# Products of two neighbouring tokens shared through differences, in 64-column tiles, in the head of a one-core transformer block

## The chip, the core and the metric

One of the cores of a Trainium2 chip runs the kernel. The metric is the device time of one execution, in microseconds, from the runs' own clock; the trace adds, for one profiled execution, when each engine's instructions and each transfer ran.

## What is computed

The reference takes x (8 x 64 channels x 128 times x 64 variables), cuts the time axis into 16 overlapping patches of 16 steps at stride 8 (the last one repeats the edge value), applies a real FFT to each patch, and maps all frequencies and channels to 64 numbers per token with W:

```
patches = xp[:, :, idx, :]                     # 16 patches of 16, stride 8
xf = jnp.fft.rfft(patches, axis=-2, norm='ortho')
x_emb = jnp.concatenate([x_real, x_imag], axis=-1) @ W.T      # 8192 tokens x 64
h = _layernorm(h + _L0_attn_ref(h), axis=-1)   # attention over all 8192 tokens, one head of 64
h = _layernorm(h + _L0_ffn_ref(h, ...), axis=-1)    # 8 experts, two of them per token
```

FFT and W are linear, so the token embedding is one matrix per time step of a patch. The attention normalizes each token to length one (f) and needs softmax(f f^T) f over all 8192 tokens.

## The kernel before, in words

The program is written engine by engine with semaphores; nothing is scheduled by a tool, so the order in the code is the order on each engine. It has three parts: the head (x to tokens h, their norms and f), the score phase (512 tiles of scores), and the last part (experts and layer norms).

**Head.** VectorE first folds DFT and W into `weff`: for each of four taps s a matrix of 128 x 128 in f32. The 128 rows are 64 channels for the first and 64 for the second half of a stride of 8 time steps. Columns 0 to 63 are the weights that a block of 8 steps has as the first half of a patch, columns 64 to 127 those that it has as the second half of the patch before. TensorE multiplies x of one batch b (128 rows, 16 blocks m of 64 variables, per tap) with `weff` in `product(b, q, s)`: two halves q of 512 columns, four taps s, summed in PSUM, so 8 matmuls of 128x512 in f32 for each of 8 batches. `first_products` interleaves batches 0 and 1 with the arrival of the four taps, and fills waits with `kept_busy` matmuls on the identity. `products(b)` does b = 2 to 7. ScalarE copies the result into `prod` (L715). `tokens(i)` (L433) transposes it with the identity: token n is the upper half of block n plus the lower half of block n+1, so 16 transposes for 8 token columns, and VectorE's `tokens_out` (L929) sums pairs in PSUM into h. Block 16, the edge, is one matmul more (L442).

x comes in eight loads of 2 MB, each as two DMAs of 1 MB (rows 0 to 63 on SyncE's queue, 64 to 127 on ScalarE's), into a ring of three buffers; load b+3 waits until the products of b are done (`s_prod`). GpSimd loads the edge values `xedge` when x of batch 1 has landed.

For each group i of 8 token columns follow: squares on ScalarE (`h_squares`, L705), their sum and a maximum on VectorE (`norms`, L935, L936), the power -0.5 (L312) and f = h times it (L314) on GpSimd, the rounded f on ScalarE (`high_of_f`, L709), its rest on GpSimd (L316), a DMA transpose and two swaps on SyncE's queue (`transposed`, `swapped`) into `hilo` and `lohi`, which `scores` reads. VectorE also centres the bias b2 in the head and splits it into three parts (15 small operations, L912 to L924); `tokens` waits for `s_b2`, though only `down` in the last part uses the result.

**Score phase.** For each s of 512: `scores(s)` (12 matmuls on 64x64 tiles, L462), exp on ScalarE (L840), the low part of it on VectorE (`low_part`, L949), and the sums over values on TensorE (L479, L492). `tokens(6)` and `tokens(7)` are issued behind `scores(0)`. Small work is hung into single steps by tables (`LATE_HIGHS`, `LATE_NORMS`, `beside`).

**Last part.** The experts: `up` (L561), `expand`, `weigh` (L1090), `down` (L643, two matmuls of 128x64 weights on 512 columns of f32, which write the two halves of one PSUM bank).

## Time and profile before

| | |
|---|---|
| median of 3 runs | 877.54 us (876.84 to 877.97) |
| the profiled execution | 877.67 us, span 875.9 us |
| TensorE | 858.7 us busy, 98% of the span |
| VectorE | 764.8 us, 87% |
| ScalarE | 651.2 us, 74% |
| GpSimd | 167.8 us, 19% |
| granted TensorE clock | 0.997 of full speed |
| read from HBM | 18.21 MB |

The span runs from the first to the last instruction; 1.8 us of the profiled time lie around it. Busy shares are means over all stages, so a change in the head is judged from the head's own rows.

### The profile page before, as it was taken

To read this page: it belongs to the slowest core of one execution; us is meant where nothing else is said; L and a number is where in the kernel's file an instruction comes from. 1 tells how busy PE (TensorE), PEld (TensorE's weight loads), DVE (VectorE), ACT (ScalarE), POOL (GpSimd) and SP (SyncE) were. 2 spreads that over 40 slices of the span, in tenths; PEclk is the share of its full clock that TensorE was granted. 3 is DMA by queue.
4 is the path that set the end of the run, shared out by engine and by line. 5 is a ranking of instruction groups with operands and counts; after the bars stand their busy time and mean duration, and the time that the engine had idled before them with its cause. 6 is when DMAs were issued, how large, how long until landed. Compare 5 with 4: busy or idle time off the path is not lost.

```text
span 875.9 us, 30900 instructions
## 1 busy us (share of the span) xinstructions
PE 858.7 (98%) x13408; PEld 449.7 (51%) x13408; DVE 764.8 (87%) x915; ACT 651.2 (74%) x1271; POOL 167.8 (19%) x183
## 2 busy tenths in 40 slices
PE   7999999999999999999999999999999999999995
PEld 6444666765555555555555555555555555543331
DVE  5425999999899999999998999899889999989994
ACT  0125888788788878878887887787878778878873
POOL 0145330000120000000000000000000199958323
PEclk9999999999999999999999999999999999999998
DMA  9996320000000000000000000000000000000111
GB/s 285 231 288 118 48 62 3 3 3 3 2 3 2 2 3 2 3 3 2 3 2 3 2 2 3 2 3 2 3 2 2 4 2 2 3 1 1 33 29 37
DMA packets 31783, 26.48 MB, mean 30 GB/s; under 512 B 12576, under 2 KB 29472, under 8 KB 31648
## 3 DMA queue, kind: packets, MB, share of 16 engines
q1 hardware_dynamic: 22768, 15.38, 7.6%
q10 hardware_dynamic: 8752, 8.86, 3.7%
q8 instruction: 106, 1.74, 0.9%
q0 software_dynamic: 128, 0.26, 0.2%
q14 instruction: 29, 0.24, 0.1%
HBM read 18.21 MB, written 2.10 MB: 23 GB/s over the span
## 4 chain that ended last, share of the span: by engine, by line
PE 95%; DVE 2%; ACT 1%; issue 1%; DMA 0%; POOLq 0%; DVEq 0%; POOL 0%; ACTq 0%
PE ps L462 38%; PE ps L479 26%; PE ps L492 13%; PE ps L393 6%; PE ps L561 3%; PE ps L643 3%; PE ps L505 2%; PE ps L402 1%; DVE ring L1090 1%; PE ps L573 1%; DVE ring L949 1%; DMA f<-in_L_tok_W_dram 0%; ACT ring L806 0%; PE ps L433 0%; PE ps L386 0%
## 5 line engine op out<-in xcount | busy, mean ns | idle before, releaser
L949 DVE TENSOR_TENSOR ring<-ring 128x1024 f16<-128x1024 f32 x512 | 603.1, 1230 | 43.9 <-ACT ring L840 43.6
L840 ACT ACTIVATE ring<-ps 128x1024 f32<-128x1024 f32 x512 | 519.3, 1020 | 129.5 <-PE ps L462 129.3
L462 PE MATMUL ps<-big 64*64 64x512 f16 x6144 | 376.2, 376 | 0.9 <-ACT ring L840 0.9
L479 PE MATMUL ps<-ring,fs 64*64 64x512 bf16 x4096 | 275.7, 384 | 0.0
L462 PEld LDWEIGHTS ps<-big 64*64 64x64 f16 x6144 | 178.9, 106 | 156.2 <-ACT ring L840 3.8
L479 PEld LDWEIGHTS ps<-ring,fs 64*64 64x64 f16 x4096 | 120.8, 106 | 105.1
L492 PE MATMUL ps<-ring,fs 64*64 64x512 f16 x2048 | 154.7, 376 | 0.5 <-DVE ring L949 0.3
L840 ACT ACTIVATION_READ_ACCUMULATOR ring<-ps 128x1 f32 x512 | 101.3, 198 | 0.0
L339 POOL TENSOR_SCALAR stat<-stat 128x16 f32<-128x16 f32 (+2 forms) x4 | 2.9, 724 | 449.8 <-DVE stat L998 449.5
L492 PEld LDWEIGHTS ps<-ring,fs 64*64 64x64 f16 x2048 | 60.3, 107 | 51.8 <-issue 2.7
L393 PE MATMUL ps<-ring,weff 128*128 128x512 f32 x128 | 56.7, 596 | 0.1
L806 ACT ACTIVATE ring<-ps,b1s 128x512 f32<-128x512 f32 x64 | 40.4, 682 | 17.6 <-PE ps L561 17.4
L1090 DVE TENSOR_TENSOR ring<-ring,ps 128x512 f32<-128x512 f32 x64 | 40.9, 681 | 5.6 <-ACT ring L806 4.6
L393 PEld LDWEIGHTS ps<-ring,weff 128*128 128x128 f32 x128 | 23.7, 190 | 28.0 <-issue 27.5
L715 ACT ACTIVATE sums<-ps 128x1024 f32<-128x1024 f32 x8 | 8.2, 1024 | 39.7 <-PE ps L393 39.7
L561 PE MATMUL ps<-big,w1s 64*128 64x512 f32 x128 | 35.9, 637 | 0.4
L643 PE MATMUL ps<-ring,w2s 128*64 128x512 f32 x128 | 34.1, 611 | 0.9 <-DVE ring L1090 0.9
L929 DVE TENSOR_REDUCE h<-ps 128x512 f32<-128x1024 f32 x8 | 9.7, 1219 | 24.7 <-PE ps L433 24.7
L330 POOL TENSOR_TENSOR stat<-stat 128x16 f32<-128x16 f32 (+2 forms) x4 | 5.2, 1292 | 127.8 <-DVE stat L993 127.8
L316 POOL TENSOR_TENSOR fs<-f,fs 128x512 f16<-128x512 f32 x8 | 11.6, 1452 | 39.9 <-ACT fs L709 39.9
L505 PEld LDWEIGHTS ps<-cst,sums 128*128 128x128 f32 x128 | 15.5, 191 | 7.0 <-issue 6.9
L312 POOL TENSOR_TENSOR stat<-stat,cst 128x8 f32<-128x8 f32 x8 | 15.0, 1875 | 14.6 <-DVE stat L936 14.2
(144 smaller groups left out, 461.3 us busy)
## 6 DMA issues: line engine op xcount, KB each, us to landing
ring<-in_x_dram ACTq DMA_DIRECT2D x8, 1024.0 KB, 14.5
ring<-in_x_dram SPq DMA_DIRECT2D x8, 1024.0 KB, 13.6
big<-big SPq DMA_DIRECT2D x16, 128.0 KB, 2.4
out_dram<-h SPq DMA_DIRECT2D x14, 128.0 KB, 2.4
f<-in_L_tok_W_dram SPq DMA_DIRECT2D x1, 288.0 KB, 4.3
fs<-consts_dram ACTq DMA_DIRECT2D x1, 256.0 KB, 17.0
xedge<-in_x_dram POOLq DMA_DIRECT2D x2, 128.0 KB, 6.7
w1s<-in_L_ffn_w_dram SPq DMA_DIRECT2D x2, 128.0 KB, 9.3
```

The costliest lines, as they stand in the source:

```text
L312: gt(stat[:, INV_H, sl(i)], stat[:, LEAST, sl(i)], minus_half, ALU.pow).then_inc(s_rt, 1)
L393: return mm(bank(2 * (b % 2) + q).rearrange("p (m v) -> p m v", v=V), weff[:, s, :], xring[:, b % XR, 8 * q:8 * q + 8, s, :], start=(s == ...
L462: last = mm(bank(SLOT_BANK[slot_of(s)] + r)[m:m + 64, :], of_k[r][:, 128 * k + m:128 * k + m + 64], of_q[r][:, q0 + 512 * r:q0 + 512 * r + ...
L479: last = mm(bank(sums_bank(s // NT) + half)[m:m + 64, :], fs[64 * r:64 * r + 64, s % NT, m:m + 64], probs[64 * r:64 * r + 64, s % 8, :].bi ...
L492: last = mm(bank(sums_bank(s // NT) + half)[64 * e:64 * e + 64, :], fs[64 * r:64 * r + 64, s % NT, 0:64], probs_lo[64 * r:64 * r + 64, s % ...
L505: last = mm(part_bank(x, b)[:, (D + 1) * k:(D + 1) * (k + 1)], outT[:, 128 * t:128 * t + 128], centred_both, start=True, stop=True)
L561: last = mm(bank(r), w1s[rows, 128 * i:128 * i + 128], hT[rows, BLK * y:BLK * y + BLK], start=True, stop=True)
L643: last = mm(bank(4)[64 * n:64 * n + 64, :], w2s[:, i, :], hidc[:, (2 * u + n) % 4, :], start=False, stop=(i == NPAIR - 1), skip_group_chec ...
L806: a(hid[:, (2 * u + r) % 4, :], bank(r), ACT.Gelu, bias=b1s[:, u % 4:u % 4 + 1]).then_inc(s_gelu, 1)
L840: a(probs[:, s % 8, :], bank(SLOT_BANK[slot_of(s)], 2), ACT.Exp, accum_out=rowsum[:, s:s + 1]).then_inc(s_pr, 1)
L949: tt(probs_lo[:, s % 8, :], probs[:, s % 8, :], probs[:, s % 8, :].bitcast(BF16)[:, 1:2 * QC:2], ALU.subtract).then_inc(s_lo, 1)
L1090: tt(hidc[:, i, :], hid[:, i, :], bank(2 + r), ALU.mult).then_inc(s_hw, 1)
```

## The change

- Buffers: five for x instead of three. Slot 3 lies in the memory of f and fs, slot 4 in that of `big`, both needed later; batches 5, 6 and 7 reuse slots 0, 1, 2 behind the products of batches 0, 1, 2. Each slot has room for a 17th block, the edge, which ScalarE writes (`edge`). SyncE loads the experts' weights behind all transposes instead of ahead of them. `xedge` is loaded when x of batch 0 has landed.
- Products in tiles of 64 columns: `both_rows` (a tap in full) is four matmuls with 64 weight columns each. Upper PSUM rows get the even tokens, lower rows the odd ones, and both halves of a token are summed in PSUM.
- Sharing: with A and B the two weight halves, token 2j is A x[2j] + B x[2j+1] = A (x[2j] - x[2j+1]) + (A+B) x[2j+1], and token 2j+1 is B (x[2j+2] - x[2j+1]) + (A+B) x[2j+1]. The product with A+B (`wboth`) serves both. `shared_row` is two matmuls of 512 columns on the differences and two of 256 columns on the shared part. VectorE computes the differences, 1024 per partition and tap (`differences_of`). It is done for 22 of the 24 taps of batches 2 to 7; batches 0, 1 and tap 0 of batches 6, 7 go in full.
- `tokens` has 8 transposes for i = 0, 1 and 12 for the others; ScalarE copies out the shared part (`odd_out`), and VectorE copies (i < 2) or adds.
- Scaling: f for groups 0 to 3 is made by ScalarE in 8 operations (`f_of_h`), for 4 to 7 by GpSimd; the maximum goes from VectorE to GpSimd (`inverse_norm`).
- The b2 operations move from the head into steps t < 14 of q = 6 of the score phase (`b2_step`, one each).

Where nothing is shown, lines are left out.

```diff
...
-LATE_HIGHS = {12: 5, 22: 6, 30: 7}
+LATE_HIGHS = {5: 4, 13: 5, 25: 6, 34: 7}
...
+XR = 5
+XLEN = (NM + 1) * HALF * V
+X_SLOT = (0, 1, 2, 3, 4, 0, 1, 2)
+X_TURN = (1, 1, 1, 1, 1, 2, 2, 2)
+X_BEHIND = {5: 1, 6: 2, 7: 3}
+SHARED_TAPS = [(), ()] + 4 * [(0, 1, 2, 3)] + 2 * [(1, 2, 3)]
+SHARED = [(b, s) for b in range(B) for s in SHARED_TAPS[b]]
...
+            even = x_at(b)[:, 0:NM:2, s, :]
+            return bass.AP(even.tensor, even.offset, (even.ap[0], even.ap[1], even.ap[1][:1] + (2,), even.ap[2]))
+
+        def differences(s):
+            piece = (h[:, NT - 2 * G:NT, :].rearrange("p j o -> p (j o)"), sums[:, NTOK - 2048:NTOK - 1024], sums[:, NTOK - 1024:NTOK],
+                     big[:, NTOK - 1024:NTOK])[s]
+            return piece.rearrange("p (j e v) -> p j e v", j=NM // 2, e=2)
...
             for b in range(B):
-                if b >= XR:
-                    sp.wait_ge(s_prod, b - XR + 1)
...
+                if X_SLOT[b] == 3:
+                    sp.wait_ge(s_wfold, 1)
+                if b in X_BEHIND:
+                    sp.wait_ge(s_prod, X_BEHIND[b])
+                sp.dma_start(x_at(b)[0:64, 0:NM].rearrange("p m s v -> p m (s v)"),
+                             x_h[b, 0]).then_inc(s_xb[X_SLOT[b]], 16)
+            sp.wait_ge(s_prod, X_SLOT.index(4) + 1)
+            for i in range(NG):
+                transposed(i)
+            swapped(NG - 1)
...
-            pool.wait_ge(s_xb[1], 16)
-            pool.wait_ge(s_xc[1], 16)
+            pool.wait_ge(s_xb[0], 16)
+            pool.wait_ge(s_xc[0], 16)
...
+            def inverse_norm(i):
+                pool.wait_ge(s_ss, i + 1)
+                pool_ts(stat[:, LEAST, sl(i)], stat[:, SUM_HH, sl(i)], 1e-24, None, ALU.max).then_inc(s_least, 1)
+                pool.wait_ge(s_least, i + 1)
+                gt(stat[:, INV_H, sl(i)], stat[:, LEAST, sl(i)], minus_half, ALU.pow).then_inc(s_rt, 1)
+
+            inverse_norm(0)
             for i in range(NG):
-                pool.wait_ge(s_ss, i + 1)
-                gt(stat[:, INV_H, sl(i)], stat[:, LEAST, sl(i)], minus_half, ALU.pow).then_inc(s_rt, 1)
-                pool.wait_ge(s_rt, i + 1)
-                gt(f[:, sl(i), :], h[:, sl(i), :], wide(stat[:, INV_H, sl(i)]), ALU.mult).then_inc(s_f, 1)
+                if i + 1 < NG:
+                    inverse_norm(i + 1)
+                if i + 1 >= NG // 2 and i + 1 < NG:
+                    pool.wait_ge(s_rt, i + 2)
+                    gt(f[:, sl(i + 1), :], h[:, sl(i + 1), :], wide(stat[:, INV_H, sl(i + 1)]), ALU.mult).then_inc(s_f, 1)
                 pool.wait_ge(s_fhi, i + 1)
                 gt(fs[:, sl(i), D:2 * D], f[:, sl(i), :], fs[:, sl(i), 0:D], ALU.subtract).then_inc(s_fs, 1)
...
-            def product(b, q, s):
-                return mm(bank(2 * (b % 2) + q).rearrange("p (m v) -> p m v", v=V), weff[:, s, :],
-                          xring[:, b % XR, 8 * q:8 * q + 8, s, :], start=(s == 0), stop=(s == HALF - 1))
+            def u_bank(b):
+                return bank(2 * (b % 2))
+
+            def both_rows(b, s):
+
+                x_b, out_b = x_at(b), u_bank(b)
+                first, second = weff[:, s, 0:D], weff[:, s, D:2 * D]
+                reach = NM // 2 if b >= 2 else NM // 2 - 1
+                mm(out_b[0:64, :], first, x_b[:, 0:NM:2, s, :], start=(s == 0), stop=False, skip_group_check=True)
+                mm(out_b[64:128, :], first, x_b[:, 1:NM:2, s, :], start=(s == 0), stop=False, skip_group_check=True)
+                mm(out_b[0:64, :], second, x_b[:, 1:NM:2, s, :], start=False, stop=(s == HALF - 1), skip_group_check=True)
+                return mm(out_b[64:128, 0:V * reach], second, x_b[:, 2:1 + 2 * reach:2, s, :], start=False,
+                          stop=(s == HALF - 1), skip_group_check=True)
+
+            def shared_row(b, s):
+
+                pe.wait_ge(s_diff, SHARED.index((b, s)) + 1)
+                x_b, out_b, d = x_at(b), u_bank(b), differences(s)
+                first_one = s == SHARED_TAPS[b][0]
+                for e in range(2):
+                    last = mm(out_b[64 * e:64 * e + 64, :], weff[:, s, D * e:D * e + D], d[:, :, e, :],
+                              start=(s == 0), stop=(s == HALF - 1), skip_group_check=True)
+                last.then_inc(s_taken, 1)
+                for e in range(2):
+                    last = mm(bank(2 * (b % 2) + 1)[64 * e:64 * e + 64, 0:256], wboth[:, s, :], x_b[:, 1 + 2 * e:NM:4, s, :],
+                              start=first_one, stop=(s == HALF - 1), skip_group_check=True)
+                return last
...
-                    for q in range(2):
-                        last = product(b, q, s)
+                    both_rows(b, s)
                     if s == HALF - 1:
-                        last.then_inc(s_prod, 1)
+                        if b == 0:
+                            pe.wait_ge(s_xe, 32)
+                            pe.wait_ge(s_wpad, 1)
+                        mm(u_bank(b)[64:128, V * (NM // 2 - 1):V * NM // 2], wpad[:, :], xedge[:, b, :], start=False, stop=True,
+                           skip_group_check=True).then_inc(s_prod, 1)
...
-                for q in range(2):
-                    for s in range(HALF):
-                        last = product(b, q, s)
+                if b == 2:
+                    pe.wait_ge(s_wboth, 1)
+                for s in range(HALF):
+                    last = shared_row(b, s) if s in SHARED_TAPS[b] else both_rows(b, s)
                 last.then_inc(s_prod, 1)
...
-                pe.wait_ge(s_padev, 1)
-                pe.wait_ge(s_b2, 1)
+                if i == 1:
+                    pe.wait_ge(s_b2o, 1)
...
+                if bp >= 1:
+                    for k in range(n0 // 4, n0 // 4 + 2):
+                        for r in range(2):
...
-            pe.wait_ge(s_xe, 32)
-            pe.wait_ge(s_wpad, 1)
...
             def load(b):
...
+            for b in range(3):
                 load(b)
...
+            load(3)
+            load(4)
...
+            def edge(b):
+                a(x_at(b)[:, NM, :, :], xedge[:, b, :].unsqueeze(1).to_broadcast([128, HALF, V]), ACT.Copy).then_inc(s_edge, 1)
...
+            def odd_out(i):
...
+                of_rows = bank(4 + i % 2 * 2, 2).rearrange("p (r k o) -> p r k o", r=2, o=D)[:, :, 4:6, :]
+                a(odd_part[i % 2].rearrange("p (k r) o -> p r k o", r=2), of_rows, ACT.Copy).then_inc(s_odd, 1)
...
+            def f_of_h(i):
...
+                for j in range(G * i, G * i + G):
+                    last = a(f[:, j, :], h[:, j, :], ACT.Copy, scale=stat[:, INV_H, j:j + 1])
+                last.then_inc(s_f, 1)
...
+            act.wait_ge(s_xe, 32)
+            for b in range(2, B - 1):
+                edge(b)
             for b in range(B):
                 act.wait_ge(s_prod, b + 1)
-                if b + XR < B:
-                    load(b + XR)
-                a(prod[:, b // 2, 0:NM, b % 2, :], bank(2 * (b % 2), 2).rearrange("p (m v) -> p m v", v=V),
+                for later in X_BEHIND:
+                    if X_BEHIND[later] == b + 1:
+                        load(later)
+                used = 12 if b >= 2 else 8
+                a(prod[:, b // 2, 0:used, b % 2, :], bank(2 * (b % 2), 2)[:, 0:V * used].rearrange("p (k v) -> p k v", v=V),
                   ACT.Copy).then_inc(s_prodev, 1)
                 if b == 1:
-                    act.wait_ge(s_pad, 1)
-                    a(prod[:, :, NM, :, :], bank(7).rearrange("p (b c v) -> p b c v", c=2, v=V),
-                      ACT.Copy).then_inc(s_padev, 1)
-                if b >= 2 and b % 2 == 0:
+                    act.wait_ge(s_b2c, 1)
+                    a(b2f[:, 0, :], b2_rows, ACT.Copy).then_inc(s_b2o, 1)
+                if b == 2:
+                    edge(7)
+                    h_squares(0)
+                    h_squares(1)
+                if b in (4, 6):
+                    odd_out(b - 2)
+                    odd_out(b - 1)
+                if 3 <= b <= 6:
+                    f_of_h(b - 3)
+                    high_of_f(b - 3)
+                if b in (4, 6):
                     h_squares(b - 2)
-                    if b >= 3:
-                        high_of_f(b - 3)
...
+                if s == 1:
+                    odd_out(NG - 2)
+                    odd_out(NG - 1)
...
+            red(wpad[:, :], weff[:, :, D:2 * D].rearrange("p s k -> p k s"), AX.X, ALU.add).then_inc(s_wpad, 1)
+            tt(wboth[:, :, :], weff[:, :, 0:D], weff[:, :, D:2 * D], ALU.add).then_inc(s_wboth, 1)
...
+            def differences_of(b, s):
+
+                if s == SHARED_TAPS[b][0]:
+                    dve.wait_ge(s_xb[X_SLOT[b]], 16 * X_TURN[b])
+                    dve.wait_ge(s_xc[X_SLOT[b]], 16 * X_TURN[b])
+                    dve.wait_ge(s_edge, b - 1)
+                if (b - 1, s) in SHARED:
+                    dve.wait_ge(s_taken, SHARED.index((b - 1, s)) + 1)
+                odd = x_at(b)[:, 1:NM:2, s, :].unsqueeze(2).to_broadcast([128, NM // 2, 2, V])
+                tt(differences(s), x_around(b, s), odd, ALU.subtract).then_inc(s_diff, 1)
...
-                red(h[:, 8 * i:8 * i + 8, :], bank(4 + i % 2 * 2, 2).rearrange("p (s n o) -> p n o s", s=2, o=D),
-                    AX.X, ALU.add).then_inc(s_h, 1)
+                own = bank(4 + i % 2 * 2, 2).rearrange("p (r j o) -> p j r o", r=2, o=D)[:, 0:4]
+                to = h[:, 8 * i:8 * i + 8, :].rearrange("p (j r) o -> p j r o", r=2)
+                if i < 2:
+                    cp(to, own).then_inc(s_h, 1)
+                else:
+                    dve.wait_ge(s_odd, i - 1)
+                    tt(to, own, odd_part[i % 2].unsqueeze(2).to_broadcast([128, 4, 2, D]), ALU.add).then_inc(s_h, 1)
...
-                then(red(stat[:, SUM_HH, sl], squares[:, i % 2], AX.X, ALU.add))
-                ts(stat[:, LEAST, sl], stat[:, SUM_HH, sl], 1e-24, None, ALU.max).then_inc(s_ss, 1)
...
+                red(stat[:, SUM_HH, sl], squares[:, i % 2], AX.X, ALU.add).then_inc(s_ss, 1)
+
+            for s in range(HALF):
+                differences_of(2, s)
+            for b in (3, 5, 7):
+                taps = SHARED_TAPS[b]
+                for s in taps[:-2]:
+                    differences_of(b, s)
+                tokens_out(b - 3)
+                differences_of(b, taps[-2])
                 tokens_out(b - 2)
-                norms(b - 2)
+                differences_of(b, taps[-1])
+                norms(b - 3)
+                if b < B - 1:
+                    taps = SHARED_TAPS[b + 1]
+                    differences_of(b + 1, taps[0])
+                    norms(b - 2)
+                    for s in taps[1:]:
+                        differences_of(b + 1, s)
+            norms(B - 3)
...
-                if q == NG // 2 + 1 and t == 18:
+                if q == NG // 2 + 1 and t == 14:
                     w2_centred()
+                if q == NG // 2 + 2 and t < 14:
+                    b2_step(t)
```

TensorE's stream from batch 2 on, before: (weff is the weights, ring holds x, x2 and xc2 are the two halves of the load).

```order
L393 MATMUL ps<-ring,weff 128x512 [waits s_prodev,s_xc2,s_x2]
L393 MATMUL ps<-ring,weff 128x512 x7
L433 MATMUL ps<-cst,sums 128x64 [waits s_b2,s_padev,s_prodev]
L433 MATMUL ps<-cst,sums 128x64 x15
```

The same place now; h, sums and big hold the differences of taps 0, 1 to 2 and 3:

```order
L449 MATMUL ps<-h,weff 64x512 [waits s_prodev,s_wboth,s_edge,s_diff,s_xc2,s_x2]
L449 MATMUL ps<-h,weff 64x512
L453 MATMUL ps<-ring,wboth 64x256 x2
L449 MATMUL ps<-sums,weff 64x512 [waits s_diff]
L449 MATMUL ps<-sums,weff 64x512
L453 MATMUL ps<-ring,wboth 64x256 x2
```

Each tap is two products of 512 and two of 256 columns, 64 weight columns wide, and waits for its difference.

VectorE from batch 3 on, now. Before, only L929, L935 and L936 stood here, group by group:

```order
L1023 TENSOR_TENSOR h<-both_f 128x1024 [waits s_edge,s_taken,s_xc3,s_x3]
L1023 TENSOR_TENSOR sums<-both_f 128x1024 [waits s_taken]
L1030 COPY h<-ps 128x512 [waits s_tr]
L1023 TENSOR_TENSOR sums<-both_f 128x1024 [waits s_taken]
L1030 COPY h<-ps 128x512 [waits s_tr]
L1023 TENSOR_TENSOR big<-both_f 128x1024 [waits s_taken]
L1038 TENSOR_REDUCE stat<-squares 128x8 [waits s_sqf]
L1023 TENSOR_TENSOR h<-big 128x1024 [waits s_edge,s_taken,s_xc4,s_x4]
L1038 TENSOR_REDUCE stat<-squares 128x8 [waits s_sqf]
```

The tokens' copies and the sums of squares stand between the differences, and each waits for TensorE or ScalarE.

ScalarE's start, now; before, the two loads into `both_f` and `big` were not there, and its loads of batches 3 and 4 came behind the first products:

```order
L762 DMA ring<-in_x_dram 64x16x256 x3
L767 DMA both_f<-consts_dram 128x512
L768 DMA cst<-consts_dram 128x134
L762 DMA both_f<-in_x_dram 64x16x256
L762 DMA big<-in_x_dram 64x16x256
L772 ACT_TABLE_LOAD
L772 ACTIVATE rsmall<-cst 128x1 [waits s_cst]
L775 ACTIVATE ring<-rtmp 128x256 [waits s_xe]
```

The edges (L775) stand behind the issue of both loads.

## Rows read from the trace of the kernel before

**Rows 1.** The page: busy times, and the chain that ended last by engine.

```profile
PE 858.7 (98%) x13408; PEld 449.7 (51%) x13408; DVE 764.8 (87%) x915; ACT 651.2 (74%) x1271; POOL 167.8 (19%) x183
PE 95%; DVE 2%; ACT 1%; issue 1%; DMA 0%; POOLq 0%; DVEq 0%; POOL 0%; ACTq 0%
```

**Rows 2.** Chain of work in the head and behind it: start, us, what.

```profile
31.14 0.86 PE ps L442 x2
...
32.36 7.06 PE ps L393 x16
...
40.66 14.20 PE ps L393 x32
54.86 1.15 PE ps L433 x32
...
71.07 7.08 PE ps L393 x16
78.15 0.02 issue
78.17 1.03 ACT sums L715
...
80.00 2.36 DVE h L929 x2
```

**Rows 3.** Chain in the last part: L643, two f32 matmuls of 64 columns.

```profile
792.25 0.86 PE ps L643 x4
...
795.13 1.01 PE ps L643 x4
```

**Rows 4.** Stretches: us, then busy PE, PEld, DVE, ACT, POOL; clock, DMA share, GB/s.

```profile
16.00:22.00 6.00, 6.00 (x31) 3.85 (x30) 5.74 (x12) 0.61 (x2) 0.40 (x1) 1.00 1.10 348
26.00:31.00 5.00, 5.00 (x13) 2.13 (x13) 0.00 (x0) 0.93 (x1) 0.61 (x1) 1.00 0.26 40
31.00:68.00 37.00, 36.90 (x145) 16.91 (x144) 12.86 (x27) 9.77 (x14) 13.54 (x11) 1.00 1.11 290
603.00:641.00 38.00, 38.00 (x700) 19.68 (x696) 34.84 (x31) 30.85 (x59) 0.00 (x0) 1.00 0.01 2
641.00:690.00 49.00, 49.00 (x876) 25.81 (x872) 43.40 (x43) 38.59 (x77) 0.00 (x0) 1.00 0.01 3
```

**Rows 5.** VectorE: L949 by duration (ns, min/median/max), and one after another in time.

```profile
L949 DVE TENSOR_TENSOR ring<-ring x512: 1162/1221/2184, 82.3 to 772.7; 128x1024 f16<-128x1024 f32 x171
...
91.07 5.76 DVE L949 TENSOR_TENSOR ring<-ring 128x1024 f16<-128x1024 f32 x5
```

**Rows 6.** Groups of the whole span and of 14.9 to 78 us: busy, mean ns, idle before.

```profile
L1090 DVE TENSOR_TENSOR ring<-ring,ps 128x512 f32<-128x512 f32 x64 | 40.9, 681 | 5.6 <-ACT ring L806 4.6
...
L935 DVE TENSOR_REDUCE stat<-squares 128x8 f32<-128x512 f32 x6 | 4.1, 686 | 4.2 <-ACT squares L705 4.2
L715 ACT ACTIVATE sums<-ps 128x1024 f32<-128x1024 f32 x7 | 7.2, 1024 | 37.6 <-PE ps L393 37.6
```

**Rows 7.** GpSimd and VectorE beside each other, in time: start, us.

```profile
58.03 1.15 POOL L316 TENSOR_TENSOR fs<-f,fs 128x512 f16<-128x512 f32 x1 [4.12 <-ACT fs L709]
58.18 1.02 DVE L936 TENSOR_SCALAR stat<-stat 128x8 f32<-128x8 f32 x1
...
59.29 1.63 POOL L312 TENSOR_TENSOR stat<-stat,cst 128x8 f32<-128x8 f32 x1
...
108.62 2.14 POOL L316 TENSOR_TENSOR fs<-f,fs 128x512 f16<-128x512 f32 x1 [6.44 <-ACT fs L709]
...
109.66 2.18 DVE L949 TENSOR_TENSOR ring<-ring 128x1024 f16<-128x1024 f32 x1
```

**Rows 8.** ScalarE, in time: a load's issue, four scalings, a copy.

```profile
2.52 5.66 ACTq L691 DMA_DIRECT2D ring<-in_x_dram  x1
8.22 5.90 ACTq L696 DMA_DIRECT2D fs<-consts_dram  x1
...
790.40 1.05 ACT L762 ACTIVATE f<-f,stat 128x64 f32<-128x64 f32 x4
```

More of the change, by code:

```diff
@@ L170, in tower, with x_at, x_around @@
         b1s = sb("b1s", [128, NPAIR], F32)
+        def x_at(b):
+            if X_SLOT[b] < 3:
+                slot = ring[:, X_SLOT[b] * XLEN:(X_SLOT[b] + 1) * XLEN]
+            else:
+                slot = (both_f if X_SLOT[b] == 3 else big)[:, 0:XLEN]
+            return slot.rearrange("p (m s v) -> p m s v", m=NM + 1, s=HALF)
+        def x_around(b, s):
+            even = x_at(b)[:, 0:NM:2, s, :]
[4 more added lines that the diff above has]
+            return piece.rearrange("p (j e v) -> p j e v", j=NM // 2, e=2)
         hT = big[:, 0:NTOK // 2]
@@ L270, in _ @@
                     sp.dma_start(b1s[rows], b1[half:E:2].rearrange("i k -> k i")).then_inc(s_w1r, 16)
-            for i in range(NG):
-                transposed(i)
-            swapped(NG - 1)
             for w, (g, p0, p1) in enumerate(PIECES):
@@ L690, in load @@
             def load(b):
-                act.dma_start(xring[64:128, b % XR, :, :, :].rearrange("p m s v -> p m (s v)"),
-                              x_h[b, 1]).then_inc(s_xc[b % XR], 16)
-            for b in range(XR):
+                act.dma_start(x_at(b)[64:128, 0:NM].rearrange("p m s v -> p m (s v)"),
+                              x_h[b, 1]).then_inc(s_xc[X_SLOT[b]], 16)
+            for b in range(3):
                 load(b)
@@ L1013, in w2_centred, with b2_step @@
                 tt(w2s[:, :, :], w2s[:, :, :], wide(rsmall[:, 6, 0:NPAIR], NPAIR), ALU.add).then_inc(s_w2c, 1)
+            def b2_step(k):
+                if k == 0:
+                    dve.wait_ge(s_b2o, 1)
+                    dve.wait_ge(s_self, 32)
+                    then(red(rsmall[:, 5, 0:1], b2f[:, 0, :], AX.X, ALU.add))
+                if k == 1:
+                    then(ts(rsmall[:, 6, 0:1], rsmall[:, 5, 0:1], -1.0 / D, None, ALU.mult))
+                if k == 2:
+                    then(ts(b2f[:, 0, :], b2f[:, 0, :], rsmall[:, 6, 0:1], None, ALU.add))
+                if k in (3, 5, 7):
+                    then(cp(b2p[:, k // 2 - 1, :], b2f[:, k // 2 - 1, :]))
+                if k in (4, 6):
+                    then(tt(b2f[:, k // 2 - 1, :], b2f[:, k // 2 - 2, :], b2p[:, k // 2 - 2, :], ALU.subtract))
+                n = (k - 8) // 3
+                at = PARTS * n
+                if k in (8, 11):
+                    then(ts(b2f[:, 3, :], b2p[:, 0, :], part_mask[:, at:at + 1], None, ALU.mult))
+                if k in (9, 12):
+                    then(stt(b2f[:, 3, :], b2p[:, 1, :], part_mask[:, at + 1:at + 2], b2f[:, 3, :], ALU.mult, ALU.add))
+                if k in (10, 13):
+                    then(stt(b2s[:, n, :], b2p[:, 2, :], part_mask[:, at + 2:at + 3], b2f[:, 3, :], ALU.mult, ALU.add))
+                if k == 13:
+                    nc.vector.engine_nop().then_inc(s_b2, 1)
             def final_variance(w):
```

80 lines of the change are left out of this document (35 added, 45 removed).

## The prediction

> **What bounds the kernel now.** The page comes first: TensorE is busy for 98% of the span and makes 95% of the chain that ended last [rows 1]. So whatever shortens TensorE's stream shortens the kernel, unless something else becomes late. The change touches the head, and there the chain is read piece by piece [rows 2]. Each batch's products take 7.06 to 7.08 us (16 records; an f32 matmul of 512 columns is two), two batches take 14.20, a pair of token groups takes 1.15 for 32 transposes, and the first scores come at 78.15. These pieces follow each other without a gap, so before 78.15 no load and no other engine is waited for from batch 2 on. Third, the stretches [rows 4] tell what will be waited for next: from 16 to 22 us the DMA engines are full at 348 GB/s, from 26 to 31 nearly idle (share 0.26, because three buffers are full), from 31 to 68 full again at 290 GB/s. The loads end only some 10 us ahead of the head. I take 0.2% (1.75 us) as what a measurement can tell from no change.
>
> **TensorE's stream.** A full tap of a batch is four records of 7.06/16 = 0.441 us, 1.77 us. In 64 columns a tap in full is as many streamed columns on half the array, twice: the same 1.77 if two tiles run side by side. A shared tap has 512 and 256 columns instead of twice 512, so 0.75 of it, 1.32. 22 taps x 0.44 = **9.7 us** less. That tiles of 64 columns in f32 run side by side is seen in `down`: two such matmuls of 512 columns take 0.86 to 1.01 us [rows 3], not the 1.77 that they would take in turn. The bounds come from the same two rows. At 0.86 a full tap costs 1.72 and nothing changes for the worse. At 1.01 a full tap costs 2.02 (10 of them, +2.5) and a shared one 1.52 (22, -5.5), and only 3.0 are left. I take 0.88, the price of one full-width matmul, since 1.01 belongs to a group whose neighbours use other tile shapes, and here 16 to 32 records of one shape stand in a row.
>
> Transposes: 96 in the head become 64 (16, 24, 24), at 1.15/32 = 0.036 us each, -1.15. The edge matmul's 0.86 [rows 2] becomes two of 64 columns, at the price of a few transposes, -0.7. Sum -11.5: TensorE alone would be through at **66.6** instead of 78.15.
>
> **What TensorE now waits for.** VectorE makes 22 differences of 1024 f32 elements. The nearest row is L949, two inputs of 1024: 1.22 us as median, and (5.76 - 1.22)/4 = 1.14 from start to start when they follow each other [rows 5]. That is 25.1 us. Between them stand six `tokens_out` of 512 from PSUM (0.64 to 0.68 as L1090) and four sums of squares (0.69 as L935) [rows 6], 6.7 us. They start when x of batch 2 is there, about 26.5, and the last product follows by 1.3: 26.5 + 25.1 + 6.7 + 1.3 = 59.6. So VectorE has 7 us of room in sum, though in places little: over a pair of batches it needs 8 x 1.14 + 2.7 = 11.8 us and TensorE 8 x 1.32 + 0.86 = 11.4. Its lead is the four differences of batch 2, made while TensorE does batches 0 and 1.
>
> GpSimd takes some of this room. Beside VectorE's L936 its subtraction L316 held VectorE until its own end (58.18 + 1.02 = 59.20, against 58.03 + 1.15), and an L949 took 2.18 instead of 1.22 beside another L316 [rows 7]. Three subtractions fall into the new stretch: 3 x 0.96 = 2.9 us, and VectorE would be through at 62.5, still ahead.
>
> Loads: five are left behind batch 2, 10.5 MB, and 0.26 MB of edge values. At the 290 GB/s of the stretch 31 to 68 they take 37 us, at the 348 of the stretch 16 to 22, where only x was under way, 31 [rows 4]. They now follow on the third load at 26 instead of 31, so the last x lands at 57 to 63; the weights' many small pieces are out of the way, and I take 62.5. From then TensorE needs one full and three shared taps, 5.7, and VectorE, which must make three differences with two `tokens_out` between and be 1.3 ahead of the end, 3.4 + 1.35 + 1.3 = 6.1. The head ends at **68.6**: 9.5 us earlier, of which TensorE would have given 11.5. The missing 2 us are a wait for x of batch 7.
>
> **Behind the head.** On the chain stand ScalarE's copy (1.03) and VectorE's two reductions, 2.36 [rows 2]. The copy has 12 of 16 blocks (-0.2), the transposes are 24 of 32 (-0.3), and the reductions become two additions of 0.65 (-1.1). They wait for ScalarE's first exp and `odd_out`, which come about 1.2 later than the transposes. Net -0.4.
>
> **Costed at nothing.** ScalarE's new work (per group 8 scalings, 1.05/4 = 0.26 each or 2.1 us [rows 8], five edges ahead of batch 2, the odd parts) lies in the 37.6 us that it waits for products [rows 6]. If that cover were gone, the copies of products would be late and each would cost its own length. The transposes on SyncE's queue go ahead of the weights, whose first reader is far behind; hilo and lohi of group 0 are ready about 62 to 64, and `scores(0)` needs them at 68. For later groups the score phase gives 10 us per group. The 15 b2 operations, 3.3 us, leave a place where VectorE idled; in q = 6 they meet 38.0 - 34.84 = 3.2 us of idle time in the first 38 us, and 5.6 in the next 49 [rows 4], with eight buffers of scores between. Bounds 0 and 3.3; taken as 0.
>
> **Sum.** -9.5 - 0.4 = -9.9. The profiled execution becomes 877.67 - 9.9 = 867.8; it lies 0.13 above the median of 877.54, so on the median 867.6. I say **867.7**.
>
> **Rivals.**
> - *Late supply* (0.17): x of batch 7 lands later than 63, or ScalarE is held up. For it: a load's issue held ScalarE for 5.66 and then 5.90 us [rows 8], since its queue was full, and two more loads are now issued ahead of the edges and of the first copy of products. If the second is taken only after 31, differences of batch 2 begin 5 us late and VectorE's 59.6 + 2.9 become 67.5, with local waits on top. Against it: the third load was taken at 8.18, and the queues drain 2 MB in 7 us. It gives a head end of 70.5 to 73: 870 to 872.
> - *Tile overhead* (0.06): each pair costs 1.01. 3.0 instead of 9.7, so 874. The Trainium skill's page TensorEngine Tiling (section "Tiling Modes") says that changing the tiling mode drains the engine. Here shapes change only around `kept_busy` and `tokens`, where they changed before too, and the group of [rows 3] stands amid such changes.
> - *GpSimd's lock for every operation* (0.05): the powers too (L312, 1.63 [rows 7]) hold VectorE for their whole length, four in the head, +6.5 on 62.5 = 69, and with local waits 71: 870. Against it: over 512 executions, many of them beside GpSimd, L949's median stays at 1.22 [rows 5]. The Trainium skill's page SBUF — State Buffer (section "SBUF: two separate sides") says that a VectorE operation with two SBUF inputs and a GpSimd operation lock each other out for the whole instruction. The trace agrees for GpSimd's operations on 512 elements (2.18 beside 1.22) and shows no such length beside the small ones.
> - *VectorE becomes the bound, slower* (0.05): a difference reads three strided patterns in f32 and writes f32, where L949 writes f16. VectorE's chain ends at 26.5 + 22 d + 8.0 + 2.9 = 37.4 + 22 d. It decides from d = 1.33 against 66.6 and loses everything from d = 37.4 to 78.5, **d = 1.87**. At the 2.18 of L949's slowest [rows 5] the head ends at 85.4, 6.9 late: 884. Against it: L949, L935 and L1090 all take about one element per ns, whatever their patterns and types.
> - *The sharing does not come into effect* (0.02): products wait on loads throughout, as x arrives at one batch per 7 us, about what TensorE needs now. Then only the 5 us of idle DMA at 26 to 31 come back: -5, 872.5. That is inside the range too.
>
> **How the numbers follow.** The forecast (865.4 to 869.5) has 0.65: from its bounds, TensorE never waiting (-11.9, so 865.6) and x at 63.5. The supply, lock and full-bandwidth rivals reach to 872.5 and hold 0.24. Left outside are part of the tile overhead and the slow VectorE, 0.11, and what none of them names. The range is 865.4 to 872.8. Faster by over 0.2%: 0.93; within: 0.02; slower: 0.05.
>
> **What would show it.** On TensorE's chain, batches 2 to 5 take 5.3 us each with 2 x 2 records of 512 and 2 x 2 of 256 columns per tap, 6 and 7 take 5.7, and about 2 us of wait in front of batch 7 are ended by a load. The first scores start near 68.6. Differences last 1.2 us, some 2.1 beside GpSimd. The DMA share stays near 1.1 from 8 to 62. The step on loads is wrong if TensorE waits for differences instead; the step on tiles, if a pair of 512-column matmuls takes over 0.95; the whole, if the first scores move by much more than the end of the kernel does.

## The result, and the profile after

The changed kernel takes **872.35 us** (median of 5 runs, 870.29 to 873.77), the kernel before 877.63 (876.84 to 877.97, 5 runs beside them). The ratio is 0.9942, interval 0.9931 to 0.9954: 5.1 us faster. The forecast was 867.7 in a range of 865.4 to 872.8. The sign and the range held, the range by 0.45 us at its upper end, but about half of the expected gain is missing.

The page of the profiled execution (872.53 us, span 870.7), to be held against [rows 1]:

```profile
PE 850.0 (98%) x13498; PEld 438.8 (50%) x13498; DVE 782.9 (90%) x929; ACT 660.2 (76%) x1315; POOL 183.3 (21%) x187
PE 93%; DVE 2%; ACT 2%; issue 2%; DMA 0%; POOLq 0%; DVEq 0%; ACTq 0%; POOL 0%
```

TensorE's share of the chain fell from 95% to 93%, and "issue" rose from 1% to 2%: there are now waits on the chain. The chain in the head shows one of 5.18 us (start, us, what), where [rows 2] had none:

```profile
32.09 1.01 PE ps L449 x4
33.09 0.43 PE ps L453 x4
33.53 0.86 PE ps L449 x4
...
37.63 0.60 ACT sums L810
38.23 0.12 ACTq L762
38.34 5.18 issue
43.52 0.81 ACT sums L810
...
44.53 0.63 ACT squares L781
...
45.79 1.21 DVE h L1023
```

A shared tap is L449 (512 columns, four records, 0.86 or 1.01) and L453 (256 columns, 0.43), 1.29 in all; 1.32 was forecast. The timeline of TensorE gives the starts of the batches and the idle time in front of an instruction, in brackets:

```profile
32.02 1.08 PE L449 MATMUL ps<-h,weff 128*64 128x512 f32 x4
...
38.28 0.71 PE L500 MATMUL ps<-cst,sums 64*128 64x64 f32 x16 [0.88 <-ACT sums L810]
38.92 1.08 PE L449 MATMUL ps<-h,weff 128*64 128x512 f32 x4
...
47.15 1.08 PE L449 MATMUL ps<-h,weff 128*64 128x512 f32 x4 [2.85 <-DVE h L1023]
48.03 0.65 PE L453 MATMUL ps<-big,wboth 128*64 128x256 f32 x4
48.79 1.98 PE L449 MATMUL ps<-sums,weff 128*64 128x512 f32 x4
...
51.40 1.29 PE L449 MATMUL ps<-sums,weff 128*64 128x512 f32 x4
...
52.95 1.02 PE L449 MATMUL ps<-big,weff 128*64 128x512 f32 x4
...
54.34 0.46 PE L500 MATMUL ps<-cst,sums 64*128 64x64 f32 x8
...
55.23 1.08 PE L449 MATMUL ps<-h,weff 128*64 128x512 f32 x4
...
67.17 0.64 PE L437 MATMUL ps<-ring,weff 128*64 128x512 f32 x1
...
73.34 0.84 PE L532 MATMUL ps<-big 64*64 64x512 f16 x12
```

The first scores (L532) stand at 73.34. In the same view of the kernel before they stand at 78.06, so the head is 4.7 us shorter, and the profiled execution is 5.1 us shorter. What TensorE lost against a stream of 1.29 us per shared tap without gaps: 0.88 ahead of the transposes; 2.85 ahead of batch 4; 2.03 in batch 4, which ran from 47.15 to 54.34, 7.19 instead of 4 x 1.29 = 5.16; 0.21 in batch 5; 0.54 in batch 7 (67.17 to 73.34, 6.17 instead of 1.76 + 3 x 1.29 = 5.63). Sum 6.5, and 73.3 - 6.5 = 66.8.

Who was late is seen in ScalarE's timeline:

```profile
30.08 0.57 ACTq L762 DMA_DIRECT2D ring<-in_x_dram  x1
30.69 0.60 ACT L810 ACTIVATE sums<-ps 128x512 f32<-128x512 f32 x1 [4.09 <-PE ps L475]
31.80 5.79 ACTq L762 DMA_DIRECT2D ring<-in_x_dram  x1
37.63 0.60 ACT L810 ACTIVATE sums<-ps 128x512 f32<-128x512 f32 x1 [6.34 <-PE ps L453]
37.68 5.79 ACTq L762 DMA_DIRECT2D ring<-in_x_dram  x1
...
43.52 0.81 ACT L810 ACTIVATE sums<-ps 128x768 f32<-128x768 f32 x1 [5.18 <-issue]
```

VectorE, in the same view:

```profile
45.19 0.69 DVE L1038 TENSOR_REDUCE stat<-squares 128x8 f32<-128x512 f32 x1 [2.85 <-ACT squares L781]
45.79 1.21 DVE L1023 TENSOR_TENSOR h<-big 128x1024 f32<-128x1024 f32 x1
...
47.52 2.35 DVE L1023 TENSOR_TENSOR sums<-big 128x1024 f32<-128x1024 f32 x2
```

ScalarE issues its half of load 6 (rows 64 to 127) ahead of the copy of batch 1, and that of load 7 ahead of the copy of batch 2. Each issue holds it for 5.79 us, where that of load 5 takes 0.57. So the copy of batch 1 starts at 37.63 instead of at about 31.8, and the copy of batch 2 at 43.52. ScalarE's squares come behind that copy, VectorE's sum of squares (L1038) waits for them, and behind it in VectorE's order stands the difference of batch 4, tap 0, for which TensorE waits. The bracket at 37.63 names L453, a product of batch 2; the copy needs the products of batch 1, which were through before 32.02, when batch 2 began. So it was the issue that held it.

The stretches (columns as in [rows 4]):

```profile
31.00:40.00 9.00, 8.12 (x61) 3.70 (x59) 6.60 (x7) 1.00 (x3) 0.00 (x0) 1.00 1.09 346
...
47.15:48.00 0.85, 0.85 (x4) 0.37 (x6) 0.85 (x2) 0.00 (x0) 0.81 (x1) 1.00 1.10 349
48.00:50.00 2.00, 1.90 (x10) 0.71 (x8) 2.00 (x3) 1.10 (x5) 1.96 (x2) 0.63 1.09 348
50.00:52.00 2.00, 2.00 (x8) 0.71 (x6) 2.00 (x2) 1.54 (x5) 1.95 (x1) 0.52 1.09 345
52.00:60.00 8.00, 8.00 (x68) 3.64 (x66) 5.63 (x8) 4.92 (x14) 2.41 (x3) 1.00 1.09 251
60.00:68.00 8.00, 8.00 (x66) 3.60 (x64) 5.34 (x6) 4.88 (x14) 7.83 (x6) 1.00 0.10 24
601.00:640.00 39.00, 39.00 (x704) 20.43 (x700) 37.95 (x43) 30.89 (x60) 0.00 (x0) 1.00 0.01 3
```

Behind the wait of 2.85 us TensorE's granted clock is 0.63 and then 0.52, so near 1.2 instead of 2.4 GHz for a while. That is 1.6 of the 2.03 us of batch 4: the taps that start at 48.79 and 51.40 take 2.61 and 1.55 instead of 1.29. The first tap of batch 4 ran before, at a clock of 1.00 (47.15 to 48.00); it takes 1.64 to the start of the next, since that next one waits for the second difference, which VectorE makes from 47.52 to about 48.7. Loads run at 345 to 348 GB/s and are through by 60. In q = 6 (601 to 640) VectorE is busy for 37.95 of 39 us and TensorE for all of it.

### The profile page after: what moved, and what is told of

It reads as the page before. It is cut to its first block, busy times and chain, and to the rows that moved or that the text cites. A ratio compares the mean times of both kernels' runs of the same rounds, so it can differ in the third digit from the quotient of the medians.

```text
span 870.7 us, 31169 instructions
## 1 busy us (share of the span) xinstructions
PE 850.0 (98%) x13498; PEld 438.8 (50%) x13498; DVE 782.9 (90%) x929; ACT 660.2 (76%) x1315; POOL 183.3 (21%) x187
## 3 DMA queue, kind: packets, MB, share of 16 engines
q8 instruction: 107, 1.75, 0.8%
## 4 chain that ended last, share of the span: by engine, by line
PE 93%; DVE 2%; ACT 2%; issue 2%; DMA 0%; POOLq 0%; DVEq 0%; ACTq 0%; POOL 0%
PE ps L532 38%; PE ps L549 26%; PE ps L562 13%; PE ps L631 3%; PE ps L714 3%; PE ps L575 2%; PE ps L449 2%; PE ps L463 1%; ACT ring L943 1%; PE ps L453 1%; PE ps L437 1%; DVE ring L1232 1%; PE ps L643 1%; PE ps L439 1%; ACT ring L906 0%
## 5 line engine op out<-in xcount | busy, mean ns | idle before, releaser
L532 PE MATMUL ps<-big 64*64 64x512 f16 x6144 | 376.3, 376 | 1.3 <-ACT ring L943 0.9
L549 PE MATMUL ps<-ring,both_f 64*64 64x512 bf16 x4096 | 275.3, 384 | 0.0
L532 PEld LDWEIGHTS ps<-big 64*64 64x64 f16 x6144 | 176.1, 106 | 159.5 <-ACT ring L943 5.5
L549 PEld LDWEIGHTS ps<-ring,both_f 64*64 64x64 f16 x4096 | 119.1, 106 | 106.8
L562 PE MATMUL ps<-ring,both_f 64*64 64x512 f16 x2048 | 154.3, 376 | 0.1
L562 PEld LDWEIGHTS ps<-ring,both_f 64*64 64x64 f16 x2048 | 59.7, 107 | 51.9 <-issue 1.9
L810 ACT ACTIVATE sums<-ps 128x768 f32<-128x768 f32 (+1 forms) x8 | 6.1, 756 | 22.6 <-PE ps L453 13.3
L341 POOL TENSOR_SCALAR stat<-stat 128x8 f32<-128x8 f32 x8 | 12.1, 1518 | 34.1 <-DVE stat L1038 34.1
L575 PE MATMUL ps<-cst,sums 128*128 128x65 f32 x128 | 17.7, 281 | 0.0
L862 ACT ACTIVATE both_f<-both_f,stat 128x64 f32<-128x64 f32 x64 | 17.3, 341 | 0.0
L353 POOL TENSOR_TENSOR both_f<-both_f 128x512 f16<-128x512 f32 x8 | 15.9, 1987 | 4.5 <-ACT both_f L799 4.5
```

Of the source, the lines that this page charges most:

```text
L532: last = mm(bank(SLOT_BANK[slot_of(s)] + r)[m:m + 64, :], of_k[r][:, 128 * k + m:128 * k + m + 64], of_q[r][:, q0 + 512 * r:q0 + 512 * r + ...
L549: last = mm(bank(sums_bank(s // NT) + half)[m:m + 64, :], fs[64 * r:64 * r + 64, s % NT, m:m + 64], probs[64 * r:64 * r + 64, s % 8, :].bi ...
L562: last = mm(bank(sums_bank(s // NT) + half)[64 * e:64 * e + 64, :], fs[64 * r:64 * r + 64, s % NT, 0:64], probs_lo[64 * r:64 * r + 64, s % ...
L575: last = mm(part_bank(x, b)[:, (D + 1) * k:(D + 1) * (k + 1)], outT[:, 128 * t:128 * t + 128], centred_both, start=True, stop=True)
L862: last = a(f[:, j, :], f[:, j, :], ACT.Copy, scale=stat[:, OF_S, j:j + 1])
```

## The experiments

My theory after this reading was that the held issues and the clock behind the wait cost the missing 4.7 us (872.35 - 867.7), and that the sharing itself works as reckoned. Rivals: the gain comes from the earlier loads alone; the loads are the bound; VectorE and GpSimd hold each other.

**The issues taken from ScalarE** (e1_loads_on_sp; base: the change)

```diff
                 sp.dma_start(x_at(b)[0:64, ...], x_h[b, 0]).then_inc(s_xb[X_SLOT[b]], 16)
+                if b in X_BEHIND:
+                    sp.dma_start(x_at(b)[64:128, ...], x_h[b, 1]).then_inc(s_xc[X_SLOT[b]], 16)
...
-                for later in X_BEHIND:
-                    if X_BEHIND[later] == b + 1:
-                        load(later)
```

> The changed kernel with both halves of the loads of batches 5, 6 and 7 issued on SyncE's queue; ScalarE issues none of them. Theory (A): the changed kernel loses its missing gain because the issue of the loads of batches 6 and 7 holds ScalarE for 5.79 us each (31.80 and 37.68), so the copies of batches 1 and 2 and the squares of group 0 come late, TensorE idles 0.9 and 2.85 us and then runs at half clock from 48 to 52. Then the first scores come at 67 to 69 instead of 73.3 and the time is 866 to 868.5. Rival (B): VectorE's chain with its local waits is the bound anyway; the first scores stay after 72 and the time at 871 or more. Rival (C): one queue for both halves carries less than two; x of batch 6 or 7 becomes late and TensorE waits for a load, 869 to 872.

Measured: 880.99 us (878.99 to 881.85), ratio 1.0041 (1.0028 to 1.0053). The copy of batch 2 came in time, at 36.54. But the loads became slow (stretch 44 to 48, and the clock behind TensorE's waits from 52 on):

```profile
44.00:48.00 4.00, 3.11 (x18) 1.34 (x20) 4.00 (x5) 2.65 (x9) 2.65 (x3) 1.00 1.13 197
...
52.00:60.00 8.00, 5.32 (x18) 2.35 (x20) 6.42 (x7) 3.68 (x11) 0.17 (x1) 0.60 1.14 195
```

The DMA engines are as full as before (share 1.13) and move 197 GB/s instead of 347. Holding ScalarE is cured, and a worse wait, for x, takes its place; the first scores come at 81.07. That is the mechanism of rival C at a higher price than it named. So this run does not decide on the theory. Whether one queue or one half of the rows at a time is slow is taken up in the last experiment.

**TensorE kept busy ahead of batch 4** (e2_busy_wait; base: the change)

```diff
                 loaded(b)
+                if b == 4:
+                    for i in range(24):
+                        mm(bank(7)[:, 256:384], ident, ident, start=True, stop=True)
```

> The changed kernel with 24 matmuls of the identity (128x128) in front of the products of batch 4, so that TensorE works through its wait for the first difference. If the granted clock of 0.63 and 0.52 between 48 and 52 us comes from the idle 2.85 us before it, it stays at 1.00 there, batch 4 takes about 1.8 us less and the time is 870 to 871.5 with less spread between runs. If the drop has another cause, it stays and the time is 872 to 873.5 (the 24 matmuls fill only idle time).

Measured: 872.98 us (872.38 to 873.43), ratio 0.9951 (0.9938 to 0.9963), the same as the change. TensorE's timeline:

```profile
44.02 5.62 PE L484 MATMUL ps<-cst 128*128 128x128 f32 x48
49.58 1.08 PE L449 MATMUL ps<-h,weff 128*64 128x512 f32 x4
...
54.89 0.46 PE L503 MATMUL ps<-cst,sums 64*128 64x64 f32 x8
```

The clock stays at 1.00 in every stretch from 26 to 76, and batch 4 takes 54.89 - 49.58 = 5.31 us instead of 7.19. So the drop of the clock came from the wait. Of the 1.88 us, 0.30 are not the clock's: the filler also gave VectorE time, and the second difference is ready. The filler is 2.4 us too long (batch 4 begins at 49.58 instead of 47.15), which eats the gain; the time alone lies where the rival had it, and the trace is what decides.

**Loads 3 to 7 held back as with three buffers** (e3_three_at_once; base: the change)

```diff
-X_BEHIND = {5: 1, 6: 2, 7: 3}
+X_BEHIND = {3: 1, 4: 2, 5: 3, 6: 4, 7: 5}
...
-            load(3)
-            load(4)
```

> The changed kernel with loads 3 to 7 held back as three buffers would hold them (3 behind the products of batch 0, 4 behind batch 1 and so on), the same slots. It tells what the early loads are worth. Theory: no issue of a load holds ScalarE, but the DMA engines idle from 26 to 31 and every x comes 5 us later or waits for products; TensorE waits for loads, the first scores come at 72 to 76, time 871 to 875. Rival: if early loads bring nothing and the hold is all, the first scores come at 68 to 70 and the time is 867 to 869.

Measured: 877.11 us (876.56 to 879.54), ratio 1.0007 (0.9997 to 1.0016).

```profile
26.00:31.00 5.00, 5.00 (x30) 3.09 (x26) 1.97 (x2) 0.60 (x1) 0.61 (x1) 1.00 0.14 25
...
40.00:44.00 4.00, 0.79 (x2) 0.33 (x4) 2.16 (x2) 0.00 (x0) 0.00 (x0) 0.50 1.10 348
```

The DMA engines idle from 26 to 31 (25 GB/s), x of batch 3 is there at 41.8, TensorE waits 5.55 us, and the clock falls to 0.50 behind it. The first scores stand at 77.31. From load 3 on every issue on ScalarE takes 0.56 or 0.57 us, yet nothing is gained: all of the change together is worth nothing while x comes as late as before. What sharing alone is worth under these loads was not run.

**The loads on SyncE, without sharing** (e4_not_shared; base: the first experiment)

```diff
-SHARED_TAPS = [(), ()] + 4 * [(0, 1, 2, 3)] + 2 * [(1, 2, 3)]
+SHARED_TAPS = 8 * [()]
```

and the differences, the shared columns of the copy, their transposes and `odd_out` dropped.

> The kernel of the first run of this call without sharing: all 24 taps of batches 2 to 7 in full, four matmuls of 64 columns, no differences on VectorE, no shared part. It tells what sharing is worth. Theory: TensorE's stream grows by 22 x 0.44 = 9.7 us and nothing else is waited for, so the first scores come at 75 to 77.5 and the time is 875 to 877. Rival: if the loads bound the head instead, it grows by less than 5 us over the first run.

Measured: 879.54 us (877.81 to 880.5), ratio 1.0026 (1.0017 to 1.0035), 1.5 us less than with sharing, at intervals that overlap. The first scores come at 79.27, where the first experiment had them at 81.07; the 9.7 us more that the theory expected did not come. TensorE waits for loads ahead of batches 6 and 7 here too, since it has the slow loads of the first experiment. It says only that while TensorE waits for such loads the sharing gains nothing.

**The same issues, later in ScalarE's order** (e6_late_issue; base: the change)

```diff
                 act.wait_ge(s_prod, b + 1)
-                for later in X_BEHIND:
-                    if X_BEHIND[later] == b + 1:
-                        load(later)
+                if b == 0:
+                    load(5)
...
                   ACT.Copy).then_inc(s_prodev, 1)
+                if b == 2:
+                    load(6)
+                if b == 3:
+                    load(7)
```

> The changed kernel with ScalarE's half of load 6 issued behind the copy of batch 2 and that of load 7 behind the copy of batch 3, each on its own queue as before. Theory: a load is taken at once when only two others are open on its queue, and both queues stay in work (about 346 GB/s), so ScalarE is held for 0.6 us each; the copies of batches 1 and 2 come at 31 and 37.5, TensorE idles neither 2.85 us before batch 4 nor runs at half clock. First scores at 67 to 69, time 866 to 868.5. Rival: ScalarE's queue falls behind SyncE's, the stretches on one queue run at 200 GB/s and TensorE waits for x of batch 7; first scores after 71, time 870 or more.

Measured: **868.46 us** (867.23 to 868.86), ratio 0.9897 (0.9883 to 0.9912), clear of the change's interval. ScalarE's timeline:

```profile
37.29 0.81 ACT L809 ACTIVATE sums<-ps 128x768 f32<-128x768 f32 x1 [4.94 <-PE ps L453]
37.29 0.54 ACTq L762 DMA_DIRECT2D ring<-in_x_dram  x1
43.24 0.81 ACT L809 ACTIVATE sums<-ps 128x768 f32<-128x768 f32 x1 [2.13 <-PE ps L453]
43.24 0.54 ACTq L762 DMA_DIRECT2D ring<-in_x_dram  x1
```

and TensorE's, at batch 4:

```profile
43.45 1.08 PE L449 MATMUL ps<-h,weff 128*64 128x512 f32 x4 [0.26 <-DVE h L1026]
...
45.09 1.08 PE L449 MATMUL ps<-sums,weff 128*64 128x512 f32 x4
```

The issues take 0.54 instead of 5.79. The DMA rate stays at 346 to 348 GB/s up to 52, the clock at 1.00, and the first scores stand at 67.97, 5.4 earlier. The first tap of batch 4 takes 1.64 here too, at full clock, which shows that this piece was no loss of the clock. The theory is confirmed: the place of two issues in the order gives back 3.9 of the missing 4.7 us (872.35 to 868.46).

**The same without sharing** (e7_late_not_shared; base: the late issues, with the edit of e4_not_shared)

> The kernel of e6_late_issue without sharing (all taps in full, no differences, no shared part). Theory: TensorE's stream alone sets the head, so it grows by 22 x 0.43 = 9.5 us: first scores at 76 to 78, time 875.5 to 877.5, which is the kernel before give or take 1 us. Rival: the head would be bound by loads or VectorE in e6_late_issue, and then this is less than 6 us slower than it.

Measured: 873.91 us (872.94 to 873.97), ratio 0.9959 (0.9945 to 0.9974). First scores at 74.50. So the sharing is worth 0.0062 of 877, 5.4 us of time, and 6.5 us of the head. I had expected 9.5; the rival had said less than 6 us of time, for a head bound by loads or by VectorE. TensorE does wait for VectorE with sharing, but that is the smaller part of what is missing. Where the rest is: 22 taps x (1.75 - 1.29) = 10.1 us; but batch 2 began at 31.86 with and at 30.76 without sharing, 1.1, from loads at the start; two groups of transposes cost 0.89 instead of 0.64, 0.5; and with sharing TensorE's batches take 1.8 us more than 1.29 per tap, about 1.2 of them waits for differences (batches 4, 5 and 7), while here it waits for nothing. Before against this kernel, 3.6 us of head are gained without sharing: batch 2 begins 1.5 earlier (30.76 against 32.29), the transposes are half (three times 0.64 against 1.14 to 1.31, 1.7 in all), and the six batches take 41.8 together instead of 42.2.

**One difference of batch 7 moved forward** (e8_order_of_7; base: the late issues)

```diff
-                for s in taps[:-2]:
+                for s in taps[:-2] if b < 7 else taps[:-1]:
                     differences_of(b, s)
                 tokens_out(b - 3)
-                differences_of(b, taps[-2])
+                if b < 7:
+                    differences_of(b, taps[-2])
```

> The kernel of e6_late_issue with VectorE's difference of tap 2 of batch 7 ahead of tokens_out(4), whose odd part comes from ScalarE behind the copy of batch 6. Theory: TensorE then no longer waits 0.2 to 0.7 us for the last differences, -0.5 us against e6_late_issue. Rival: tokens_out and the norms behind it come later and the start of the scores gives it back, no difference (within 0.3 us).

Measured: **867.29 us** (866.47 to 868.49), ratio 0.9891 (0.9875 to 0.9908): the fastest median, and faster than both kernels, but not told apart from 0.9897. The first scores stand at 66.69, of which 1.0 comes from an earlier batch 2 (30.86 against 31.86) and 0.3 from batch 7. Behind them a wait opens that neither the change nor the late issues had in this place:

```profile
76.86 0.63 PE L562 MATMUL ps<-ring,both_f 64*64 64x512 f16 x8 [0.81 <-DVE ring L1070]
```

**All scaling on GpSimd** (e9_f_on_gpsimd; base: the late issues)

```diff
+            pool.wait_ge(s_rt, 1)
+            pool.wait_ge(s_prod, 4)
+            gt(f[:, sl(0), :], h[:, sl(0), :], wide(stat[:, INV_H, sl(0)]), ALU.mult).then_inc(s_f, 1)
...
-                if i + 1 >= NG // 2 and i + 1 < NG:
+                if i + 1 < NG:
...
-                    f_of_h(b - 3)
```

> The kernel of e6_late_issue with f of all groups on GpSimd, as before the change, and none on ScalarE. Theory: the split of the scaling is worth little by itself, since ScalarE and GpSimd are both ahead of need: within 0.5 us of e6_late_issue. Rival: each GpSimd operation on 512 elements holds VectorE for about 1 us (1.92 instead of 1.22 beside one in the changed kernel), four more of them cost the differences 1 to 4 us, 868 to 871.

Measured: 868.17 us (866.07 to 869.59), ratio 0.9895 (0.9875 to 0.9914), no difference. The split of the scaling is worth nothing that can be measured here.

**Both queues on the same half of the rows** (e10_same_half; base: the late issues). From load 3 on each queue has half of the blocks of all rows, first rows 0 to 63, then 64 to 127:

```diff
+                    for r in range(2):
+                        sp.dma_start(x_at(b)[64 * r:64 * r + 64, 0:8]..., x_h[b, r][:, 0:8])
...
+                    for r in range(2):
+                        act.dma_start(x_at(b)[64 * r:64 * r + 64, 8:16]..., x_h[b, r][:, 8:16])
```

> Base is the kernel of e6_late_issue. From load 3 on both queues carry the same rows of a load at about the same time: SyncE's the first eight blocks of rows 0 to 63 and then of rows 64 to 127, ScalarE's the last eight blocks of both in the same order. Bytes and number of queues stay as they are. Theory A, it was the number of queues: in e1 200 GB/s were all that one queue gets; here two are in work, so the rate from 31 to 56 stays at 346 to 348 GB/s, first scores at 67 to 69, 867 to 869 us. Theory B, it was the rows: transfers to rows of one half alone get 200 GB/s however many queues carry them. Then the rate lies at 200 to 260 between 31 and 68 (more where the queues have drifted apart), TensorE waits for loads before batches 5 to 7, first scores at 73 to 80, 872 to 880 us.

Measured: 886.15 us in one run beside 878.38 for the kernel before, slower than theory B had it, with the first scores at 86.62. Stretches:

```profile
36.00:40.00 4.00, 1.03 (x4) 0.48 (x6) 0.28 (x1) 1.20 (x3) 0.00 (x0) 0.50 1.13 210
...
44.00:48.00 4.00, 4.00 (x38) 1.96 (x36) 2.00 (x4) 0.81 (x1) 0.00 (x0) 1.00 1.13 197
```

Two queues are in work, and yet 189 to 216 GB/s at a share of 1.13 to 1.15. So the first experiment lost its rate because one half of the rows was carried at a time; a second queue on the same half does not bring it back. One queue that carries both halves at once was not tried. Which end does it, the 64 rows in SBUF or the alternate blocks in HBM that make up one half, was not tried. The Trainium skill's page DMA: Bandwidth & Descriptors (section "Rules for kernel authors") says that two transfers to disjoint partition halves serialize; here they do not, at 347 GB/s side by side against 200 alone, and the measurement decides. The single transfer over all 128 rows that the page advises instead was not run.

## Why the prediction was right, and where it was wrong

**TensorE's stream: right in sum.** 66.6 was forecast for TensorE alone; 66.8 is what remains after its losses. Two errors offset each other in it: a shared tap takes 1.29, not 1.32, and the edge brought about 0.3 (batch 2 begins at 32.02 instead of 32.29), not 0.7. That the run with the moved difference has its first scores at 66.69 is chance: its batch 2 began 1.2 us earlier, and it still waits for differences. The pair of tiles costs 0.86 to 1.01, the lower of the two bounds nearly throughout, so *Tile overhead* falls.

**"Costed at nothing" failed.** The step let ScalarE's work lie in the 37.6 us that it waits for products, and said that without this cover each late copy would cost its own length. It counted ScalarE's operations and not its load issues, though [rows 8] had shown issues of 5.66 and 5.90 us. Two of 5.79 now stand ahead of copies, and they cost 0.88 + 2.85 us of waiting and 1.6 us of clock, 5.3. Moved by a few lines they cost next to nothing: from the start of batch 2 to the first scores it is 36.11 us (31.86 to 67.97) instead of 41.32, 5.2 less. The rival *Late supply* had this mechanism ("ScalarE is held up") and, within 0.4 us, the time (870 to 872), but put it at the loads ahead of the edges. Those did no harm: differences of batch 2 began at 28.98, 2.5 later than reckoned, and were still in time.

**The clock was missing altogether.** No term priced what a wait of TensorE costs behind its end. Here 2.85 us of waiting cost 1.6 us more.

**The loads were mis-sized.** "The missing 2 us are a wait for x of batch 7" did not come. The 290 GB/s of [rows 4] were taken as a rate for x; they are a mean over a stretch. Measured are 345 to 348 GB/s from 31 to 52, and at 60 the loads are through, with no wait for x behind batch 2. These 2 us too much offset part of the 6.5 us of losses: 68.6 - 66.6 = 2.0 expected, 6.5 found, and the difference of 4.5 is nearly all of 872.35 - 867.7 = 4.65. That is luck: without the wait that was reckoned and did not come, the forecast would have been near 865.7 and the miss 6.7. And 872.35 lies outside the forecast's own bounds (865.4 to 869.5); it is inside the range only because the range was stretched to 872.8 for the rivals.

**VectorE: right in sum, with local waits.** A difference takes 1.21 to 1.23 us and 1.14 from start to start. *VectorE becomes the bound* falls. GpSimd was expected to hold VectorE for 2.9 us; of the 22 differences two are longer, 1.63 (at 30.12, beside a cast on GpSimd) and 1.92 (at 68.20), 1.1 in all. Mostly it is the other way round (GpSimd's timeline of the change, beside and without differences):

```profile
59.89 1.14 POOL L341 TENSOR_SCALAR stat<-stat 128x8 f32<-128x8 f32 x1 [5.59 <-DVE stat L1038]
...
65.92 0.24 POOL L341 TENSOR_SCALAR stat<-stat 128x8 f32<-128x8 f32 x1
```

The same maximum takes 1.14 us beside a difference (VectorE's from 59.72 to 60.94, the maximum from 59.89 to 61.03) and 0.24 alone. So where the two meet it is mostly GpSimd that is held, and *GpSimd's lock for every operation* falls as a cost to VectorE. The Trainium skill's page SBUF — State Buffer (section "SBUF: two separate sides") has a lock that the loser waits out for the whole instruction, and by that rule the trace agrees.

**Behind the head: right as far as can be told.** First scores 4.7 earlier, the profiled execution 5.1: -0.4, as forecast. It is one pair of executions, and those of one kernel lie up to 3.5 us apart (870.29 to 873.77). **b2 operations: right.** They filled VectorE's idle time in q = 6 (34.84 of 38 before, 37.95 of 39 now), and TensorE waited for none of it.

**Sharing does not take effect** fell by the size of its own term, but its mechanism is near: with the late loads of the third experiment the whole change brought nothing, with slow loads the sharing nothing, and with the late issues the sharing 5.4 us.

## What to carry to other kernels

An engine that issues loads is an engine with a load's issue in its order: count it as work of up to its longest row, and put it behind, not ahead of, what others wait for. A wait in TensorE's stream is to be priced with the clock behind it, here 1.6 us on top of 2.85. A mean rate over a long stretch is no rate of a transfer; take it from a stretch in which that transfer alone is under way.
